# A one-core decoder layer: transfers that start on shifted engines, loads in pairs, twelve tile statistics on ScalarE, and a group of selects placed earlier on GpSimd

## What is computed

```python
def _L0_attn_ref(x, log_A, B_param, C_param, D_param, log_dt, ln_gamma, ln_beta, W_out, b_out):
    residual = x
    xn = layernorm(x) * ln_gamma + ln_beta
    dt = exp(log_dt); dA = exp(-exp(log_A) * dt[:, None]); dB = B_param * dt[:, None]
    def step(h, u):                       # h: batch x 256 channels x 64 states
        h = dA * h + dB * u[..., None]
        return (h, einsum('dn,bdn->bd', C_param, h) + D_param * u)
    ys = scan(step, 0, xn over the 1024 tokens)
    return residual + einsum('btd,ed->bte', ys, W_out) + b_out
x = x + _L0_attn_ref(_layernorm(x, axis=-1), ...)
x = x + _L0_xattn_ref(ctx_1024, ctx_1024, _layernorm(x, axis=-1), ...)   # 16 heads, 64 keys
x = x + _L0_ffn_ref(_layernorm(x, axis=-1), ...)                         # 256 -> 1024 -> 1024 -> 1024 -> 256
```

## Time and profile before

| | us |
|---|---|
| median of three runs | 923.99 |
| the three runs | 923.17, 923.99, 926.75 |
| the profiled execution | 926.07 |
| its span | 924.3 |
| TensorE busy in the span | 876.2 |
| DMA share of the whole span / from 36 to 60 us | 0.19 / 1.03 |

### The profile page before, as it was taken

The page is one execution under the profiler, slowest core; times in us unless marked ns, Lnnn a source line. Parts: engine busy times, 40 slices in busy tenths (PEclk is TensorE's granted clock), DMA queues, the critical chain, the costliest instruction groups (busy, mean ns, idle before and its releaser), DMA issues.

```text
span 924.3 us, 15870 instructions
## 1 busy us (share of the span) xinstructions
PE 876.2 (95%) x5960; PEld 710.9 (77%) x5960; DVE 511.6 (55%) x926; ACT 487.3 (53%) x772; POOL 189.0 (20%) x212
## 2 busy tenths in 40 slices
PE   1669998999999999999999999999999999999998
PEld 0369876778877788777877787778777887788887
DVE  7855486455456455555565565555555466454422
ACT  5728442576256734663475536753576256734432
POOL 5777400500050003200230014000500040003000
PEclk9779999999999999999999999999999999999999
DMA  9880996500110002000200010001100110001000
GB/s 337 210 194 5 312 401 250 228 1 1 52 45 0 0 26 71 0 0 23 74 0 0 0 67 29 0 0 52 45 0 0 51 45 0 0 23 45 1 1 24
DMA packets 15166, 60.37 MB, mean 65 GB/s; under 512 B 2757, under 2 KB 4554, under 8 KB 14314
## 3 DMA queue, kind: packets, MB, share of 16 engines
q1 hardware_dynamic: 15098, 59.87, 18.9%
q0 software_dynamic: 32, 0.00, 0.0%
HBM read 48.19 MB, written 23.20 MB: 77 GB/s over the span
## 4 chain that ended last, share of the span: by engine, by line
PE 83%; DVE 8%; issue 6%; ACT 2%; DVEq 0%; POOL 0%; DMA 0%; SPq 0%; POOLq 0%
PE pair L1427 45%; PE pair L1414 9%; PE pair L1439 6%; PE pair L1453 4%; PE pair L1356 4%; PE pair L1367 3%; PE pair L1383 3%; PE pair L546 2%; PE pair L553 2%; PE pair L1376 2%; PE pair L560 1%; PE pair L1323 1%; PE pair L618 1%; DVE vbuf L1229 1%; DVE prob L1219 1%
## 5 line engine op out<-in xcount | busy, mean ns | idle before, releaser
L1031 ACT ACTIVATE vbuf<-pair,scl 128x512 f32<-128x512 f32 x128 | 87.7, 685 | 230.7 <-PE pair L1427 227.5
L1427 PE MATMUL pair<-h2hi,h_turned 128*128 128x512 f32 x512 | 202.6, 396 | 0.0
L1427 PE MATMUL pair<-h2lo,h_turned 128*128 128x512 f32 x512 | 199.5, 390 | 0.0
L1427 PE MATMUL pair<-h1hi,h_turned 128*128 128x512 f32 x384 | 153.3, 399 | 0.0
L1427 PE MATMUL pair<-h1lo,h_turned 128*128 128x512 f32 x384 | 150.0, 391 | 0.0
L1193 DVE TENSOR_TENSOR h1lo<-vbuf,h1hi 128x512 fp32r<-128x512 f32 x80 | 57.8, 722 | 119.5 <-ACT h1hi L1032 118.7
L1427 PEld LDWEIGHTS pair<-h2hi,h_turned 128*128 128x128 f32 x512 | 96.1, 188 | 25.2 <-issue 5.9
L1427 PEld LDWEIGHTS pair<-h2lo,h_turned 128*128 128x128 f32 x512 | 96.2, 188 | 19.3
L1193 DVE TENSOR_TENSOR h2lo<-vbuf,h2hi 128x512 fp32r<-128x512 f32 x64 | 44.3, 691 | 106.9 <-ACT h2hi L1032 106.7
L1414 PE MATMUL pair<-zThi,w_turned 128*128 128x512 f32 x224 | 91.7, 409 | 4.0 <-DVE vbuf L1229 3.9
L1427 PEld LDWEIGHTS pair<-h1hi,h_turned 128*128 128x128 f32 x384 | 72.1, 188 | 24.7 <-issue 10.5
(11 more groups left out here) (168 smaller groups left out, 1634.9 us busy)
## 6 DMA issues: line engine op xcount, KB each, us to landing
h_turned<-d_h SPq DMA_DIRECT2D x2, 4096.0 KB, 15.9
xres<-in_x SPq DMA_DIRECT2D x8, 512.0 KB, 6.9
tok<-in_xs SPq DMA_DIRECT2D x8, 512.0 KB, 11.6
xr<-x_rows SPq DMA_DIRECT2D x8, 512.0 KB, 3.5
out<-xr SPq DMA_DIRECT2D x16, 256.0 KB, 2.0
x_rows<-xres SPq DMA_DIRECT2D x7, 512.0 KB, 13.3
x_rows<-x1t SPq DMA_DIRECT2D x7, 512.0 KB, 2.6
w_turned<-d_w SPq DMA_DIRECT2D x3, 1024.0 KB, 18.1
```

The source lines that it names most:

```text
L1031: e.activation(vb[:, s % 2, :], h_ps[s % 4], ACT.Gelu, scale=sc)
L1427: ins = e.matmul(bank, w[:, k, m * P:(m + 1) * P], src[part][:, k, :], start=(k == 0 and part == 0), stop=(k == HC - 1 and part == 1))
```

## The change

The change has four parts, all in the mixer.

1. `tt_load` loads two groups at a time, 8 KB for each partition. The very first of these loads is cut in two: its first 32 partitions are read with a source written as 8 times 4 rows, the other 32 with a source of 32 rows. All other loads keep 64 partitions. The entries' loads for groups 2 and 3, and 5 and 6, are paired too. The order is now kernel rows 0-1, 2-3, entries 5-6, kernel rows 4-5, entries 7, kernel rows 6-7. The bytes stay the same.
2. ScalarE takes the statistics of twelve tiles, VectorE of twenty; VectorE's break for `spreads(0)` stands after six tiles.
3. Of the second half's 32 slices of `tok`, ScalarE takes 15 instead of 16, VectorE 17.
4. The two selects of group 0 stand ahead of the power `rsm` on GpSimd.

```diff
-ACT_SHARE = (19, 16)
-ACT_UPTO = (19, 35)
-ACT_STATS = (8, 16)
+ACT_SHARE = (19, 15)
+ACT_UPTO = (19, 34)
+ACT_STATS = (8, 20)
...
     def tt_load(e, g):
+        span = 2 * GRP * PAD
+        dst = ring[:, GRP * PAD * g:GRP * PAD * (g + 2)] if g < 4 else ttw[g // 2 - 2][:, :]
         for h in range(2):
-            e.dma_start(TT[g % 8][L * h:L * h + L, :],
-                        bass.AP(t["kr_h"], (8 * h + g) * (GRP * PAD), [[1, L], [1, GRP * PAD]])).then_inc(xr_T_in[g % 8], 16)
-
-    def entries_load(e, g):
+            at = (8 * h + g) * (GRP * PAD)
+            if g == 0 and h == 0:
+                e.dma_start(dst[0:32, :], bass.AP(t["kr_h"], at, [[4, 8], [1, 4], [1, span]])).then_inc(xr_T_in[0], 16)
+                e.dma_start(dst[32:64, :], bass.AP(t["kr_h"], at + 32, [[1, 32], [1, span]])).then_inc(xr_T_in[0], 16)
+            else:
+                e.dma_start(dst[L * h:L * h + L, :], bass.AP(t["kr_h"], at, [[1, L], [1, span]])).then_inc(xr_T_in[g], 16)
+
+    def entries_load(e, g, n=1):
...
-        for g in range(NGRP):
-            if g == 6:
-                e.wait_ge(nat_v, 1)
-            tt_load(e, g)
-            if g in (1, 3, 5):
-                entries_load(e, (5, 6, 7)[g // 2])
+        tt_load(e, 0)
+        tt_load(e, 2)
+        entries_load(e, 5, 2)
+        tt_load(e, 4)
+        entries_load(e, 7)
+        e.wait_ge(nat_v, 1)
+        tt_load(e, 6)
...
     def mask(e, g):
-        e.wait_ge(xr_T_in[g], 48)
+        e.wait_ge(xr_T_in[g // 2 * 2], 64 if g < 2 else 48)
...
         e.wait_ge(g_back, 2)
+        mask(e, 0)
+        e.wait_ge(t_mask, 2)
         e.wait_ge(nat_v, 1)
         e.wait_ge(powd, 2)
         e.tensor_tensor(rsm[:, :], svn[:, :], mhalf[:, :], ALU.pow).then_inc(natural, 1)
...
     def gpsimd_core(e):
-        for g in range(NGRP):
+        for g in range(1, NGRP):
             mask(e, g)
...
-        stats(SB, SB + 7)
+        stats(ACT_STATS[1], ACT_STATS[1] + 6)
         spreads(0)
-        stats(SB + 7, TILES)
+        stats(ACT_STATS[1] + 6, TILES)
```

22 lines of the change are left out of this document (10 added, 12 removed).

## The result

The changed kernel took 927.23 us (median of 20 runs, 924.86 to 930.88), the kernel before, beside it, 925.17 (20 runs, 922.86 to 926.75). The ratio is 1.002, 95% interval 1.0012 to 1.0028: slower by some 2 us, where 7.3 us less had been forecast; the difference is small but clear of its interval. The forecast, 916.7, and its range, 914.4 to 921.5, both lie under what came.

The account below looks back on a forecast made before the run. TensorE was taken to bound the kernel, stopping twice at 36 to 60 us beside full DMA engines. Pass 3 ending at 58.6 against 65.82, plus 0.1, gave 7.3 us: median 916.7, range 914.4 to 921.5.

Parts of the forecast that it names:

- Part 1: Statistics and split of tok between ScalarE and VectorE: state products start 3.0 us earlier, at 40.9.
- Part 2: Mixer loads: first pair lands at 39.3 (38.7 to 40.6), all loads end by 52.5 instead of about 64.
- the offset: Half the DMA engines run one transfer ahead, both partition halves are written together: about 408 GB/s instead of 233.
- Part 3: Selects on GpSimd: group 0 ready at 42.2 at no cost, group 1 at 51.8, a new wait of 4.5 us.
- Pass 2: TensorE's mixer pass starting in effect at 51.8 instead of 54.8, taking 3.6 us at half clock.
- Part 4: TensorE's stops are instruction blocks queued behind full DMA engines; first ends at 52.3, second's 3.65 us go.
- the second stop: TensorE's 3.65 us stop, restarting at 63.73; forecast to go, its block asked for at about 52 with the queue nearly empty.
- the wait for group 1: TensorE waits 4.5 us for group 1's selects, behind power and head mask on GpSimd, until 51.8.
- The sum: Pass 3 ends at 58.6 against 65.82, with 0.1 for pass 4: 7.3 us gained; forecast chance 0.60.
- the first stop: TensorE's 4.47 us stop ending at 55.32; forecast to end at 52.3, running at once with the selects' wait.
- A: Rival: the offset does nothing, loads stay at 233 GB/s, the second stop stays; 3.1 us gained, median 920.9; chance 0.26.
- B: Rival: blocks wait longer behind 8 KB rows, rate stays 233; 2.8 us slower, 926.8; chance 0.06.

Follow-up runs that it names:

- split: Kernel before with only the new statistics and slices (ScalarE twelve tiles and 15 slices, VectorE twenty and 17); ratio 0.9985.
- both: Kernel before with the new statistics and slices and group 0's selects ahead of the power, without the paired loads; ratio 0.9993.
- eight: Changed kernel with the first 32 rows' source written with strides 1 and 8, so its two levels aren't merged; ratio 1.0029 to the kernel before.
- pairs: Kernel before with only the paired loads and their order; statistics, slices and selects as before; ratio 1.0017.
- hold: Kernel before with kernel rows 2 and up held until octet 1's state products, rows 4 and up and weights until octet 2 is done; ratio 0.9994.
- shallow: Kernel before with each group's kernel rows (from group 2) issued only when the previous group's have landed, weights after the last; ratio 0.9974.
- gated: Kernel before with kernel rows from group 3 on tied to TensorE's progress, two octets apart, and the weights after octet 11; ratio 0.9994.

## Why the prediction was wrong, point by point

**Part 1 was right in its waits, and lucky in its time.** The first product came at 40.61, forecast 40.9. ScalarE's third round of statistics fitted into its idle time, and VectorE's second addition waited for ScalarE, as worked out. But the 17 slices took 4.45 us and not 3.9, and the addition 1.23 and not 1.9, since the selects came at 43.05 and not at 39.3. Where selects ran earlier the start was worth less: 42.08 in "split", 41.94 in "both".

**Part 2 failed, and the forecast with it, in four steps.**
- That the offset happens. It didn't: the builder merged 8 by 4 rows into 32. The prediction read the source line and not what is built of it. This could have been seen beforehand, in the built program.
- That with half the engines one transfer ahead the rate is about 408. In "eight", whose source keeps its two levels, it was 221 GB/s; with distinct rows, 241. Whether the engines did run apart there, no row shows. The odds of two to one for the partitions rested on one coincidence, 233 being little more than half of 408. The runs bear the partitions out only as far as 128 of them reach 358 to 382; the cure doesn't follow from it.
- That the first pair lands at 39.3, at 40.6 at the latest. It landed at 42.9. The bound took the landings of 256 KB transfers, 4.7 us at most, for a transfer of 512 KB behind 512 KB more. At 220 GB/s 1.05 MB take 4.8 us and not 2.6, but that isn't the whole of it: from 34 to 40 us the engines moved 172 GB/s, 1.03 MB and so about the size of the pair, yet it landed only at 42.9, when they had moved 1.7 MB. So other transfers took part of the rate beside it (an estimate from these sums), and neither bound has that.
- 8 KB rows were costed at nothing, but the rate fell (219 against 230 GB/s in "pairs"), and the queue drained at about 67 us and not at 64, where Part 2 had 52.5. Parts 3 and 4 needed the earlier hour.

**Part 3 had the mechanism and missed its start.** Group 0 was ready at 46.3 instead of 42.2: its selects began at 43.05 instead of 39.3, by the landing above (0.8 us of it because SyncE issued the first load at 34.3 and not at 33.5), and took 3.23 instead of 2.9. TensorE waited 3.87 us for what had been costed at nothing, or at 1.0 with the latest landing. From there the chain was as forecast: power 5.43, head mask, two selects, group 1 ready at 56.3, where 51.8 had been forecast. Pass 2 ended at 59.95 instead of 55.4, so the 3.3 us of the earlier start were gone, with 1.5 more.

**Part 4 was right in what the stops are, and wrong that the second would go.** An empty queue at the time of asking takes a stop away ("hold", octet 1 in 2.6 us). But the prediction misread the kernel before: it took the packet between 64 and 65 us for the next one after 52 to 53, and there is another between them, from 60 to 61 us:

```profile
q8 instruction: 1, 0.02, 6.6%
```

That one belongs to the second stop, and it came in a full queue. In the changed kernel the packet of the first block came while TensorE waited for the selects anyway; these are the rows of q8 for 53 to 54 and 62 to 64 us:

```profile
q8 instruction: 1, 0.02, 8.2%
```

```profile
q8 instruction: 1, 0.02, 3.7%
```

In the kernel before each stop ended 2.8 us after its packet had started (52.5 and 60.9). In the changed kernel the first packet started at 53.25, so by that (an estimate) the block alone would have held TensorE to about 56.1, and the wait for group 1, to 56.37, cost only some 0.3 us more. The second packet came in a queue that was still full, since nothing had become faster, and the stop stayed at 3.77 us. The point that the prediction overlooked is what "shallow", "hold" and "gated" show: TensorE asks every few microseconds, and in each of the three placements most of what was taken from one stop came back in others.

**The sum.** Of the 7.3 us forecast at the mixer's end, -1.1 came. The start gave 3.3. The wait for group 0 took 3.9, and the one for group 1 ran in place of the first stop and ended 1.05 us later than it (56.37 against 55.32); the second stop stayed. That these waits are the loss is true of this execution up to octet 2 (0.7 us behind before); "eight", with 1.8 us less of the first wait, still ended octet 15 at 100.27. The other 1.6 us of the profiled execution go with the longer half clock behind 162 us; the prediction took all later work to move along unchanged. The level was off as well: the 2.08 us between profiled execution and median came from three runs, and over twenty it is 0.9, so the same gain would have read 917.9.

**The rivals.** A had the right rate, the one that stays, but priced only that: 920.9 needed the first pair ready as early as with the forecast. B gave nearly the right time, 926.8, by luck and for a wrong reason: with 8 KB rows the blocks didn't wait twice as long (4.47 became 4.71 in "pairs"). No rival had the pair itself arriving late.

**What stays open.** Why 64-partition rows are slow; why the paired loads cost 2.4 us only behind octet 2 (in "pairs"; "eight" shows the same). In "pairs" and in "split" the later octets have small stops that the kernel before doesn't have. The waits of TensorE in "split" from 64 to 100 us (total, times, longest):

```profile
PE pair L552 <- issue: 1.1, 3, 0.5
```

Octet 2 is 2.3 us earlier there and octet 15 0.3 us later. Whether that comes from where the blocks fall in the octets wasn't tested.

## What to carry to other kernels

Where a trick rests on the levels of an access pattern, look at the pattern in the built program: levels that describe one even list are merged. When a load is made larger, ask first what the first consumer now waits for, and price the landing from transfers as large, in a queue as full: the rate alone gives about 40 us here, and it was 42.9. When a part is timed alone, look at what its neighbours do to it: 1.5 us of this start came from a select that was late. And before tuning transfers around a TensorE that runs from a long unrolled program, look for stops that end with "issue" beside a full DMA queue: issuing loads only one group ahead was worth 0.9974 here, against 0.9985 and 0.9987 for the best parts of the change, whose intervals overlap with it.
